# A test-time-training recurrence on one core: a chunk's query output moves into the next chunk's fourth round, GpSimd's work goes between the rounds, and the second weight to be renormalised is the small one

## The reference, cut to what matters

```python
def step(carry, xs):
    W0, W1, W2 = carry
    qi, ki, vi, li = xs
    gq = silu(jnp.einsum('bhd,bcd->bhc', W0, qi))
    hq = jnp.einsum('bhd,bcd->bhc', W2, qi)
    o = jnp.einsum('boh,bhc->bco', W1, gq * hq)
    gba = jnp.einsum('bhd,bcd->bhc', W0, ki)
    hbm = jnp.einsum('bhd,bcd->bhc', W2, ki)
    ...
    dw0, dw1, dw2 = (newton_schulz5(dw0), newton_schulz5(dw1), newton_schulz5(dw2))
    W0 = renorm(W0 + dw0, n0)
    W1 = renorm(W1 + dw1, n1)
    W2 = renorm(W2 + dw2, n2)
    return ((W0, W1, W2), o)

def newton_schulz5(G):
    X = X / (jnp.linalg.norm(X, axis=(1, 2), keepdims=True) + 1e-07)
    for a, b, c in NS_COEFFS:
        A = X @ jnp.swapaxes(X, 1, 2)
        Bm = b * A + c * (A @ A)
        X = a * X + Bm @ X
```

## Time and profile before

| | |
|---|---|
| median of 3 runs | 1979.29 us (1974.09 to 1983.97) |
| the profiled execution | 1982.01 us, span of its instructions 1980.3 us |
| share of the span in which PE, DVE, ACT, POOL are busy | 88%, 70%, 40%, 55% |
| the recurrence | from about 16 to 258 us of the span |
| granted TensorE clock, mean of the span | 0.914 of full speed |
| granted TensorE clock in the recurrence, and behind it | 0.75, 0.94 |

### The profile page before, as it was taken

One profiled execution on the slowest core, in us unless ns is written; L12 is line 12 of the kernel. 1 busy time (PEld: TensorE's weight loads), 2 busy tenths in 40 slices (PEclk: granted clock), 3 DMA queues, 4 the chain that ended last, 5 costly groups with the idle time before them and its releaser, 6 DMA issues.

```text
span 1980.3 us, 35242 instructions
## 1 busy us (share of the span) xinstructions
PE 1745.4 (88%) x13630; PEld 948.8 (48%) x13630; DVE 1392.0 (70%) x2440; ACT 792.9 (40%) x1181; POOL 1095.0 (55%) x644
## 2 busy tenths in 40 slices
PE   4888751948999999999999999999999999995893
PEld 3666641834444444444444444444444444443482
DVE  3666654347787777887777877778778887786474
ACT  3444420533444444444444444444444444441131
POOL 2232204032777677776767767777677777682303
PEclk8886755969999999999999999999999999996897
DMA  7000000210000000000000000000000000003122
GB/s 243 4 3 3 3 1 30 62 38 1 1 1 1 1 1 1 1 1 1 1 1 1 1 1 1 1 1 1 1 1 1 1 1 1 1 1 99 32 58 60
DMA packets 41533, 32.76 MB, mean 17 GB/s; under 512 B 3604, under 2 KB 37392, under 8 KB 41368
## 3 DMA queue, kind: packets, MB, share of 16 engines
q1 hardware_dynamic: 31096, 22.12, 3.6%
q0 software_dynamic: 2048, 4.20, 0.7%
q10 hardware_dynamic: 8224, 4.19, 0.7%
HBM read 18.96 MB, written 11.53 MB: 15 GB/s over the span
## 4 chain that ended last, share of the span: by engine, by line
PE 81%; DVE 9%; issue 5%; POOL 3%; ACT 1%; DMA 1%; SPq 0%; DVEq 0%; POOLq 0%; ACTq 0%
PE psum L1781 23%; PE psum L1766 20%; PE psum L1740 8%; PE psum L1760 6%; PE psum L1407 2%; PE psum L1796 2%; PE psum L1790 2%; PE psum L1181 1%; PE psum L1713 1%; PE psum L1193 1%; PE psum L1367 1%; DVE a_mx L1945 1%; POOL a_acc L2077 1%; PE psum L1417 1%; PE psum L447 1%
## 5 line engine op out<-in xcount | busy, mean ns | idle before, releaser
L2077 POOL TENSOR_TENSOR a_acc<-a_acc,a_Pb 128x832 f32<-128x832 f32 x448 | 893.3, 1994 | 307.8 <-ACT a_Pb L1883 275.1
L1945 DVE TENSOR_REDUCE a_mx<-psum 128x2 f32<-128x1024 f32 x512 | 625.5, 1224 | 237.2 <-PE psum L1740 234.2
L1883 ACT ACTIVATE a_Pb<-psum 128x1024 f32<-128x1024 f32 x512 | 496.7, 1022 | 703.5 <-PE psum L1766 701.5
L1781 PE MATMUL psum<-a_Pb,a_Vb 128*64 128x512 f32 x2048 | 494.3, 604 | 0.0
L1996 DVE TENSOR_TENSOR a_acc<-a_acc,a_Pb 128x192 f32<-128x192 f32 x448 | 230.9, 515 | 28.9 <-ACT a_Pb L1883 5.4
L1781 PEld LDWEIGHTS psum<-a_Pb,a_Vb 128*64 128x64 f32 x2048 | 127.2, 136 | 244.7 <-issue 173.7
L1740 PE MATMUL psum<-a_Kh,a_Qh 64*128 64x512 f32 x1024 | 231.3, 447 | 8.4 <-DVE a_mx L1945 8.3
L1766 PE MATMUL psum<-a_Qh,a_Kh 64*128 64x512 f32 x1024 | 231.1, 447 | 0.0
L1766 PE MATMUL psum<-a_Ql,a_Kh 64*128 64x512 f32 x1024 | 203.8, 393 | 0.0
L1740 PEld LDWEIGHTS psum<-a_Kh,a_Qh 64*128 64x128 f32 x1024 | 97.1, 184 | 222.6 <-issue 211.6
L1766 PE MATMUL psum<-a_Qh,a_Kl 64*128 64x512 f32 x1024 | 203.4, 392 | 0.0
(11 more groups left out here) (385 smaller groups left out, 2004.0 us busy)
## 6 DMA issues: line engine op xcount, KB each, us to landing
x_rows<-zero ACTq DMA_DIRECT2D x2, 2048.0 KB, 20.9
g_w<-in_L_ffn_w_eDF_dram SPq DMA_DIRECT2D x2, 1408.0 KB, 8.7
r_W<-in_L_ffn_W_dram SPq DMA_DIRECT2D x1, 2048.0 KB, 12.4
r_tile_x<-x_rows SPq DMA_DIRECT2D x16, 128.0 KB, 2.1
y_rows<-r_tile_y SPq DMA_DIRECT2D x16, 128.0 KB, 1.8
g_tile_x<-x_rows SPq DMA_DIRECT2D x16, 128.0 KB, 2.2
y_rows<-g_tile_y SPq DMA_DIRECT2D x16, 128.0 KB, 1.8
g_w<-in_L_ffn_w_eFD_dram SPq DMA_DIRECT2D x2, 512.0 KB, 10.5
```

The lines of the kernel that those rows point to most:

```text
L1781: last = pe.matmul(ps[HEAD[h], B_O, :], b.Vb[:, p // 2 % 2, kc, at], b.Pb[:, step % BUFS, h * QT:(h + 1) * QT], start=(kc == 0), stop=(kc ...
L1883: act.activation(b.Pb[:, step % BUFS, :], ps[:, slot:slot + 2, :].rearrange("p a b -> p (a b)"), ACT.Exp, scale=SCALE).then_inc(S["probs"], 1)
L1945: v.tensor_reduce(b.mx[:, :, qc, quarter:quarter + 1], ps[:, bank:bank + 2, :], AX.X, ALU.max).then_inc(S[f"free{bank}"], 1)
L2077: g.tensor_tensor(b.acc[:, u, at], before, b.Pb[:, step % BUFS, at], ALU.add).then_inc(S["added_pool"], 1)
```

## The change

The output of chunk c-1 is issued by PE in round 3 of chunk c, between L436 and L447, instead of in its head; `t.W1T` has two buffers for it. It is written to another bank, the one from which L481 takes the values, and waits for L481. ScalarE copies it to a new tile `t.o` after the rounds (`keep_output`), GpSimd adds the input a chunk later, and VectorE takes the statistics in round 2 (`stats`).

The weights are renormalised in the order 0, 2, 1 and the products of the next head follow it; the rounds go through the weights in the order 0, 1, 2. GpSimd's gate is cut in two parts and its scaling by rates in three: each part is issued once the last G of a round is there. ScalarE takes the gate's sigmoid behind the copies of the products, and the roots ahead of the query copies.

```diff
@@ forward_output @@
         if c:
-            pe.wait_ge(S["residual"], c)
+            pe.wait_ge(S["output_kept"], c)
+        if c + 3 < NC:
+            pe.wait_ge(S["v_out"], c + 4)
         for i in range(TPC):
             for g in range(2):
-                last = pe.matmul(ps[:, B_OUT, 256 + i * P:256 + (i + 1) * P], t.hq[:, g, i * P:(i + 1) * P], t.W1T[:, g, :], start=(g == 0), stop=(g == 1))
+                last = pe.matmul(output_at(ps, c)[:, i * P:(i + 1) * P], t.hq[:, g, i * P:(i + 1) * P], t.W1T[:, c % 2, g, :], start=(g == 0), stop=(g == 1))
@@ ttt_pe @@
-        parts = ((0, t.k0s[:, u], t.dg), (2, t.v1s[:, u], t.hd), (1, t.k2s[:, u], t.dh))
+        parts = ((0, t.k0s[:, u], t.dg), (1, t.k2s[:, u], t.dh), (2, t.v1s[:, u], t.hd))
         products(c)
         pe.wait_ge(S["slope"], c + 1)
         query_products(c)
-        if c:
-            forward_output(c - 1)
...
+            if it == 3 and c:
+                forward_output(c - 1)
             if it < NI - 1:
@@ ttt_act @@
     for c in range(NC - 1):
-        if c:
-            gate(c - 1)
         act.wait_ge(S["products"], 3 * c + 1)
         act.activation(t.sig[:, :, :], products_at(ps, 0), ACT.Sigmoid).then_inc(S["products_out"], 1)
         act.wait_ge(S["products"], 3 * c + 3)
+        act.activation(t.db[:, :, :], products_at(ps, 2), ACT.Copy).then_inc(S["products_out"], 1)
         act.activation(t.hb[:, :, :], products_at(ps, 1), ACT.Copy).then_inc(S["products_out"], 1)
-        act.activation(t.db[:, :, :], products_at(ps, 2), ACT.Copy).then_inc(S["products_out"], 1)
+        if c:
+            gate(c - 1)
...
+        roots(c + 1)
         act.wait_ge(S["q_products"], c + 1)
         act.activation(t.gq[:, c % 2], q_products_at(ps, 0), ACT.Copy)
         act.activation(t.uq[:, c % 2], q_products_at(ps, 1), ACT.Copy).then_inc(S["q_out"], 1)
-        roots(c + 1)
...
+        if c:
+            keep_output(c - 1)
         keep_w1(c)
@@ ttt_dve @@
+            if it == 2 and c > 1:
+                stats(c - 2)
@@ ttt_pool @@
     for c in range(NC - 1):
-        if c:
-            gate(c - 1)
         g.wait_ge(S["gated"], c + 1)
         g.wait_ge(S["products_out"], 3 * c + 2)
+        g.tensor_tensor(t.dh[:, :, :], t.db[:, :, :], t.sg[:, :, :], ALU.mult).then_inc(S["hidden"], 1)
+        g.wait_ge(S["products_out"], 3 * c + 3)
         g.tensor_tensor(t.hd[:, :, :], t.sg[:, :, :], t.hb[:, :, :], ALU.mult).then_inc(S["hidden"], 1)
-        g.wait_ge(S["products_out"], 3 * c + 3)
-        g.tensor_tensor(t.dh[:, :, :], t.db[:, :, :], t.sg[:, :, :], ALU.mult).then_inc(S["hidden"], 1)
         scale(c + 1)
-        if c < NC - 2:
-            rates(c + 1)
-        if c:
-            blocks(c)
-    gate(NC - 2)
+        if c > 1:
+            residual(c - 2)
+        for it in range(NI - 1):
+            g.wait_ge(S["G"], 15 * c + 3 * it + 3)
+            if it < 2 and c:
+                gate(c - 1, it)
+            if it < 3 and c < NC - 2:
+                rate(c + 1, it)
+            if it == 3 and c:
+                blocks(c)
+    gate(NC - 2, 0)
+    gate(NC - 2, 1)
```

More of the change, by code:

```diff
@@ L217 @@
 B_Q, B_KV, B_OUT, B_RATES = 0, 4, 3, 7
+PRODUCT_ORDER = (0, 2, 1)
 NS_BANK = (4, 5, 6)
 GRAD_BANK, XT_BANK, SUM_BANK, W1T_BANK, X_BANK = 7, 2, 2, 2, 7
-NS_ORDER = (0, 2, 1)
+NS_ORDER = (0, 1, 2)
 def qkv_bank(c):
@@ L315, in products @@
                 pe.wait_ge(S["weighed"], c + 2)
-        for m in range(3):
+        for n, m in enumerate(PRODUCT_ORDER):
             if c:
-                pe.wait_ge(S["moved"], 3 * (c - 1) + m + 1)
-            elif m == 1:
+                pe.wait_ge(S["moved"], 3 * (c - 1) + n + 1)
+                if n == 1:
+                    pe.wait_ge(S["norms"], 3 * c + 2)
+            elif n == 1:
                 pe.wait_ge(S["v_out"], 2)
@@ L455, in ttt_pe @@
                 pe.wait_ge(S["X"], 7 * c + 7)
-                for m in range(3):
-                    pe.wait_ge(S["G"], at + (1 if m == 0 else 3))
+                for n, m in enumerate(PRODUCT_ORDER):
+                    pe.wait_ge(S["G"], at + (1 if n == 0 else 3))
                     for h in range(HEADS):
@@ L575, in ttt_act @@
     keep_w1(NC - 1)
+    keep_output(NC - 2)
+    keep_output(NC - 1)
 def ttt_dve(k):
@@ L613, in scales, with stats @@
         v.tensor_tensor(s2v, s2v, rb, ALU.mult).then_inc(S["scales"], 1)
-    def residual(c):
-        v.wait_ge(S["output"], c + 1)
-        v.tensor_tensor(k.y_all[:, TPC * c:TPC * c + TPC, :], ps[:, B_OUT, 256:512].rearrange("p (a b) -> p a b", a=TPC),
-                        k.x_all[:, TPC * c:TPC * c + TPC, :], ALU.add).then_inc(S["residual"], 1)
+    def stats(c):
         v.wait_ge(S["residual"], c + 1)
@@ L682, in ttt_dve @@
         head_squares(c + 1)
-        if c:
-            residual(c - 1)
         scales(c + 1)
@@ L746, in ttt_dve @@
     dve.wait()
+    v.wait_ge(S["output"], NC - 1)
     v.tensor_tensor(t.hq[:, :, :], q_products_at(ps, 1), t.gq[:, 1], ALU.mult).then_inc(S["q_hidden"], 1)
-    residual(NC - 1)
+    for c in range(NC - 3, NC):
+        stats(c)
 def ttt_pool(k):
@@ L779, in blocks, with gate @@
         g.tensor_tensor(t.WB[:, :, :], bcast(t.Wc[:, 2, :].unsqueeze(1), [P, HEADS, HID]), k.mask4[:, :, :], ALU.mult).then_inc(S["blocks"], 1)
-    def gate(c):
-        g.wait_ge(S["q_gate"], c + 1)
-        g.wait_ge(S["q_out"], c + 1)
-        if c:
-            g.wait_ge(S["output"], c)
-        pool.did(g.tensor_tensor(t.gq[:, c % 2], t.gq[:, c % 2], t.sigq[:, :, :], ALU.mult))
-        pool.wait()
-        g.tensor_tensor(t.hq[:, :, :], t.uq[:, c % 2], t.gq[:, c % 2], ALU.mult).then_inc(S["q_hidden"], 1)
+    def gate(c, part):
+        if part == 0:
+            g.wait_ge(S["q_gate"], c + 1)
+            g.wait_ge(S["q_out"], c + 1)
+            pool.did(g.tensor_tensor(t.gq[:, c % 2], t.gq[:, c % 2], t.sigq[:, :, :], ALU.mult))
+        else:
+            if c:
+                g.wait_ge(S["output"], c)
+            pool.wait()
+            g.tensor_tensor(t.hq[:, :, :], t.uq[:, c % 2], t.gq[:, c % 2], ALU.mult).then_inc(S["q_hidden"], 1)
     pool.did(g.memset(t.heads[:, :, :], 0.0))
@@ L798, in ttt_pool @@
     scale(0)
-    rates(0)
+    for part in range(3):
+        rate(0, part)
     for c in range(NC - 1):
-        if c:
-            gate(c - 1)
         g.wait_ge(S["gated"], c + 1)
         g.wait_ge(S["products_out"], 3 * c + 2)
+        g.tensor_tensor(t.dh[:, :, :], t.db[:, :, :], t.sg[:, :, :], ALU.mult).then_inc(S["hidden"], 1)
+        g.wait_ge(S["products_out"], 3 * c + 3)
         g.tensor_tensor(t.hd[:, :, :], t.sg[:, :, :], t.hb[:, :, :], ALU.mult).then_inc(S["hidden"], 1)
-        g.wait_ge(S["products_out"], 3 * c + 3)
-        g.tensor_tensor(t.dh[:, :, :], t.db[:, :, :], t.sg[:, :, :], ALU.mult).then_inc(S["hidden"], 1)
         scale(c + 1)
-        if c < NC - 2:
-            rates(c + 1)
-        if c:
-            blocks(c)
-    gate(NC - 2)
+        if c > 1:
+            residual(c - 2)
[9 more added lines that the diff above has]
+    gate(NC - 2, 1)
     blocks(NC - 1)
+    for c in range(NC - 3, NC):
+        residual(c)
 def norm_dve(k, n, g, have_stats=False):
```

98 lines of the change are left out of this document (53 added, 45 removed).

## The result

| | before | changed kernel |
|---|---|---|
| median of 5 timed runs each, same chip | 1979.29 us (1973.49 to 1985.16) | 1993.22 us (1988.85 to 2009.68) |
| ratio | | 1.0085, 95% interval 1.0044 to 1.0127 |
| the profiled execution, its span | 1982.0, 1980.3 us | 2009.7, 2008.3 us |
| granted clock of the recurrence (16 to 258) | 0.75 | 0.58 |

The forecast was 1968 us (1959 to 1978). The time lies outside it, on the other side of no change. The profiled execution of the changed kernel is the slowest of its five, so its trace shows the effect at its largest: 27.7 us over the profile of before, where the medians differ by 13.9.

What follows compares the result with a forecast made beforehand. The recurrence was taken as bound by a chain of engine hand-overs, none full. Per chunk -1.8 - 0.45 + 1.0 - 0.5 = -1.75, six times -10.5, total -11.5 from the median 1979.3: 1968 us, range 1959 to 1978.

Steps and rivals of the forecast that it cites:

- The clock: Rounds 3 and 4: the moved output keeps TensorE's clock up more often, 3 of 5 us saved, -0.5 a chunk.
- rival 5: Clock does not rise at the head without L349, rounds run at half clock: +31 us, 2010; chance 0.07.
- signs of being wrong: Rounds 0 to 2 clocked below 1.0 in most chunks; L722 waits for GpSimd; L362 waits for gate or values, or lasts 2.
- Head, "-1.8": Chunk head: gate and output leave it, so the last square's L545 comes earlier; -1.8 us over six chunks with an output, each.
- L742 then costs about 0.2: Chunk head: with GpSimd's gate gone, VectorE's L742 drops from 1.27 us to about 0.2.
- Round 0, "-0.45": Round 0: GpSimd's scalings leave, L706 is no longer slowed and L710 is bound by PE; -0.45 us a chunk.
- Round 3, "+1.0": Round 3: the output placed there takes 1.1 us, 0.1 of it hidden; +1.0 us a chunk, +1.7 at half clock.
- GpSimd's work "hidden": Between rounds: GpSimd's moved parts delay L706 but not L710, 0.25 us to spare; L704, reading PSUM, is held free.
- rival 4: GpSimd's work between rounds stalls L704 too: +1.3 us a chunk, leaving -3.7, 1975.6; chance 0.09.
- Clock kept up, -0.5: Rounds 3 and 4: output's full-array products keep the clock up more often, -0.5 us a chunk.
- The forecast -11.5: Whole kernel: -1.75 us a chunk, six times -10.5, with chunk 0 and the tail -11.5 in total.

Runs made afterwards that it cites:

- experiment 1: Changed kernel with unneeded full products (fillers) in the heads: two from chunk 1 1.0033, three in every chunk 0.9995, four from chunk 1 0.9983, four in every chunk 0.9952.
- Experiments 3 and 7: 3: kernel before, outputs of chunks 1 to 5 cut to 8 columns, 1.0106. 7: kernel before plus four fillers, every chunk 1.0020, chunk 0 alone 0.9974.
- experiment 5: Changed kernel with four fillers in every chunk, its round 3 output cut to 8 columns for chunks 0 to 5: 1976.63 us, ratio 0.9971.
- experiment 6: Kernel before with single parts: GpSimd's scalings by rates and blocks between the rounds, 1988.48 us; order 0, 2, 1 of renormalisation and products alone, 1986.93 us.
- the kernel with four fillers everywhere: Changed kernel with four unneeded 128x128 products between query products and turned gradients in every chunk, chunk 0 too: 1974.37 us, ratio 0.9952.
- Experiment 7: Kernel before with four fillers ahead of the output in every chunk: 1987.06 us, ratio 1.0020; with four in chunk 0 alone: 1977.23 us, ratio 0.9974.

## Why the prediction was wrong, point by point

**The step that failed** is "The clock" together with rival 5: "The clock does not rise at the head once L349 is gone", priced at +31 us and given 0.07. It is what happens. Its price was right in kind: per chunk +5.1 forecast, and 34.1 against a mean of 29.4 (chunks 0 to 5 of before, 51.53 to 227.80 in six) is +4.7. The sum itself held the clock's rise for given: for the loss of L349 it charged 0.5 us at three heads and 0.2 for L362 at half clock, and nothing for rounds 0 to 2. The profiled run is 27.7 us longer. The median, 13.9, is less, I take it since more chunks of other executions are lifted all the same (one chunk is in the profiled one); I had no term for that in between. Of the signs of being wrong that I had listed, three are in the trace: the clock in rounds 0 to 2, an L362 of 2.05 us, and its wait for the values, though of 0.19 only.

**Why I gave it 0.07.** The one argument was chunk 0 of the profile of before, which rose to 1.00 without L349. That was one observation of something that varies: in single executions of kernels whose chunk 0 has the same products in its head, it isn't lifted (33.6 and 34.1 us above, 34.0 in the run of experiment 1 with four fillers from chunk 1, 32.7 in the changed kernel). Experiments 3 and 7 show both sides of it: of five chunks without the output four stay at half clock, and the kernel gains 5 us once chunk 0 has its filler. I also weighed the output's two places unequally. I gave it power to keep the clock up in round 3, which it has (experiment 5), and none to bring it up in the head, where it had done so in every chunk of my own trace that has it.

**The rest of the sum held.**
- Head, "-1.8": from the first new weight to the last square 11.59 against 12.87 to 14.50, mean 13.6: -2.0. It hides a cost I did not count. With the small weight in the middle, the table load comes 2.42 behind the first new weight instead of 2.01, since the second column-wise sum is later: +0.4 in the renormalisation, -2.4 in the head.
- "L742 then costs about 0.2": 0.25. For this instruction the order alone would do (experiment 6); I had put it down to the gate leaving the head.
- Round 0, "-0.45": 0.36 where it stands alone.
- Round 3, "+1.0", from a length of 1.1: at full clock it lasts 1.13, and L463 (the old L447) starts 1.06 behind its start. Rows of the kernel with four fillers everywhere, chunk 2:

```profile
111.44 0.39 DVE L727 COPY t_Ab<-psum 128x32 f32<-128x32 f32 x3 [1.27 <-PE psum L440]
111.47 0.63 POOL L791 TENSOR_TENSOR t_k0s<-t_qw,t_lr 128x256 f32<-128x256 f32 x1
111.86 0.35 DVE L729 TENSOR_TENSOR t_T<-t_Ab,t_aI 128x96 f32<-128x96 f32 x1
...
112.46 0.39 DVE L733 SCALAR_TENSOR_TENSOR t_Gm<-psum,t_T 128x32 f32<-128x32 f32 x3 [0.24 <-PE psum L452]
...
117.28 0.39 ACT L498 ACTIVATE t_vv<-psum 128x256 f32<-128x256 f32 x1
...
117.81 1.13 PE L362 MATMUL psum<-t_W1T,t_hq 128*128 128x128 f32 x8
...
118.87 0.55 PE L463 MATMUL psum<-t_Gm,t_X 32*64 32x32 f32 x24
```

- GpSimd's work "hidden": L729, the old L706, takes 0.35 beside it and G still waits for PE (0.24). L727, which reads PSUM, keeps its 0.39 beside L791: rival 4 is out. The Trainium skill (SBUF — State Buffer, "Who interferes with whom") says that a VectorE instruction with at most one SBUF input, outside the two-port modes, does not contend with GpSimd, and that one with two contends with a GpSimd instruction that reads SBUF. The trace agrees: L727, which has none, takes 0.39 beside L791 as L704 does alone, and L729, which has two, 0.35 instead of 0.26.
- "Clock kept up, -0.5" in rounds 3 and 4: at full clock the output does that, and gives back about the 1.06 that it costs (experiment 5). In the changed kernel it meets half clock in chunks 2 to 6; behind it the clock is up for 3 to 4 us in chunks 2 to 5 and not at all in chunk 6.

**Does the sum hold where the clock is made to rise?** The forecast -11.5 less six fillers. A filler moves the last square from 2.77 behind the end of L343 (176.04 to 178.81) to 3.96 (102.60 to 106.56), +1.19, so +7.1: -4.4 us. Experiment 7 gives -4.4 against the kernel before with chunk 0 made sure, with some 6 us of uncertainty either way, so this fits the sum and does not prove it or its terms; that the two numbers meet is in part luck. What the change would be worth with the clock as before and no filler, no run shows.

**The range** was too narrow in kind. The terms' errors were tenths of a microsecond; the one state that the sum assumed, the clock at five rounds' start, was worth 5 us a chunk, and its chance rested on one chunk.

What stays open: why one chunk is lifted and the next is not under the same code (with three fillers, chunks took 28.5, 34.4, 27.3, 29.4, 34.9 and 27.2 us in one execution). All the profiled executions together, seven chunks each, give a count. With no filler in the head and of the output at most 8 columns, 5 of 27 chunks were lifted (the kernel with the added wait counts in); with two fillers 2 of 6, with three 5 of 7, and with four full products or more, needed or not, 58 of 58. Even then the clock can fall early: in the kernel with four fillers in every chunk it fell in round 3 of chunk 3 (146.3), and that chunk took 30.9 us. I can say what lifted it every time in these runs, and not what sets the limit.

## What to carry to other kernels

In a stretch that is a chain of small hand-overs, a block of dense matrix work is not only load: it may be what gives the stretch behind it the full clock. Before moving it, look in which slices the granted clock rises and what PE did just ahead, in every repetition and in more than one execution; then price the move with the clock of the rounds behind it, first. If the block has to go, put other work there: four products that nobody needs cost about 1.2 us of head, and with them the chunk as a whole fell from 34.1 to 27.4 us, 1.2 included.

## What the runs showed that I had not expected

- Less work can be slower: 2001.6 against 1982.3 us on the same chip for the kernel before without five of its outputs (ratio 1.0106).
- The order of the three renormalisations alone takes a VectorE instruction of 0.25 us out of a stall of 1.0 us.
- The same program's executions differ by 1% (1988.85 to 2009.68), with the mean granted clock from 0.905 down to 0.890: part of a kernel's spread is likely which chunks are lifted (only one of them has a trace). With the filler in chunk 0 the kernel before kept within 1975.7 to 1982.0 in 12 runs, while 23 runs of it without filler, on the same chip, went from 1974.5 to 1989.3.
- The mean clock of an execution, and the clock's row at its start, can mislead. With the order alone changed (experiment 6) the row says 1.00 through the whole of chunk 0, and L451 there lasts 0.86 us, as at half clock, where at full clock it is 0.55. Of the 23 runs without filler just named, the seven with the highest means, 0.923 to 0.928, took 1982.2 to 1989.3 us, and the fastest of all had 0.920. The lengths of the same products in two places tell which level it was.
